# The end of a two-layer transformer kernel: the last head period and the final norm and projection rearranged

## The reference

```python
# 32 heads, causal top-k mask; x is 1024 x 512
attn = jax.nn.softmax(scores, axis=-1)
out = jnp.einsum('bhqk,bhkd->bqhd', attn, v).reshape(b, s, H * VD)
x = x + out @ o_w
# last part: one 512 x 512 matrix, W with its low-rank terms folded in
x = x + (layernorm(x) @ (W + lora).T + bias)
```

## Time and profile before

| what | value |
|---|---|
| median of 3 runs | 1490.97 us (1489.38 to 1497.5) |
| profiled execution: its time | 1491.74 us |
| its span, first to last instruction | 1489.9 us |
| mean granted TensorE clock over the span | 0.946 |

### The profile page before, as it was taken

One profiled execution on the slowest core, in us unless ns is written; L12 is line 12 of the kernel. 1 busy time (PEld: TensorE's weight loads), 2 busy tenths in 40 slices (PEclk: granted clock), 3 DMA queues, 4 the chain that ended last, 5 costly groups with the idle time before them and its releaser, 6 DMA issues.

```text
span 1489.9 us, 21223 instructions
## 1 busy us (share of the span) xinstructions
PE 1329.6 (89%) x7144; PEld 1109.1 (74%) x7144; DVE 1113.9 (75%) x2247; ACT 823.4 (55%) x1799; POOL 629.7 (42%) x620
## 2 busy tenths in 40 slices
PE   2767999999899789997659999999999999999978
PEld 1645788888789677774358788888888888888856
DVE  5637434443657599999948988988989988898864
ACT  4554442233246466763446776666777667667631
POOL 2421110010037445544435555556665555555522
PEclk9978999999999899996579999999999999999988
DMA  6531210000212335645530000000000000000101
GB/s 217 173 99 50 88 61 1 1 19 0 66 39 70 103 88 169 211 140 182 177 113 13 1 28 28 27 28 27 27 2 28 27 28 27 28 27 15 55 25 57
DMA packets 83722, 95.59 MB, mean 64 GB/s; under 512 B 11680, under 2 KB 59296, under 8 KB 83104
## 3 DMA queue, kind: packets, MB, share of 16 engines
q1 hardware_dynamic: 83616, 94.24, 20.1%
HBM read 75.34 MB, written 18.87 MB: 63 GB/s over the span
## 4 chain that ended last, share of the span: by engine, by line
PE 66%; DVE 17%; ACT 4%; DMA 4%; issue 3%; SPq 2%; POOL 2%; DVEq 1%; ACTq 0%; POOLq 0%
PE ps L328 16%; PE ps L330 15%; PE ps L329 15%; PE ps L1691 8%; PE ps L1711 3%; DVE acc L1274 3%; PE ps L1710 3%; DVE top L1285 2%; DVE xn_l L1339 2%; DVE rop L1297 1%; DVE acc L1288 1%; DVE rop L1295 1%; DVE pm L1327 1%; DMA iwq_raw<-in_L_attn_idx_wq_w 1%; DMA wring<-in_L_ffn_w 1%
## 5 line engine op out<-in xcount | busy, mean ns | idle before, releaser
L682 POOL TENSOR_SCALAR pm<-pm,smx 128x128 f32<-128x128 f32 (+7 forms) x256 | 189.7, 750 | 218.6 <-DVE smx L1333 218.6
L1327 DVE CUSTOM_DVE_ANT_0 pm<-ps,mbias 128x128 f32<-128x128 f32 (+7 forms) x256 | 191.5, 753 | 40.8 <-PE ps L330 25.9
L941 ACT ACTIVATE pm<-pm,smx 128x128 f32<-128x128 f32 (+7 forms) x256 | 197.3, 772 | 35.8 <-DVE smx L1327 34.0
L1691 PE MATMUL ps<-ident,pm 128*128 128x128 f32 x1152 | 176.1, 278 | 9.5 <-DVE xn_l L1339 3.5
L947 ACT ACTIVATE xn_h<-ps 128x512 fp32r<-128x512 f32 (+3 forms) x256 | 128.6, 512 | 86.0 <-PE ps L1691 82.9
L1339 DVE TENSOR_TENSOR xn_l<-ps,xn_h 128x512 fp32r<-128x512 f32 (+3 forms) x256 | 144.6, 588 | 27.3 <-ACT xn_h L947 26.4
L328 PE MATMUL ps<-latT_l,qc_h 128*128 128x512 f32 (+3 forms) x384 | 142.8, 372 | 21.1 <-SPq L319 12.1
L1691 PEld LDWEIGHTS ps<-ident,pm 128*128 128x128 f32 x1152 | 133.2, 142 | 35.9 <-issue 12.7
L330 PE MATMUL ps<-latT_h,qc_h 128*128 128x512 f32 (+3 forms) x384 | 134.0, 349 | 0.0
L329 PE MATMUL ps<-latT_h,qc_l 128*128 128x512 f32 (+3 forms) x384 | 133.4, 347 | 0.0
L1274 DVE SCALAR_TENSOR_TENSOR acc<-ps,iw,acc 128x768 f32<-128x768 f32 (+4 forms) x105 | 87.9, 889 | 24.3 <-ACT ps L855 24.0
(11 more groups left out here) (271 smaller groups left out, 3695.6 us busy)
## 6 DMA issues: line engine op xcount, KB each, us to landing
iwq_raw<-in_L_attn_idx_wq_w SPq DMA_DIRECT2D x48, 256.0 KB, 3.2
base<-in_L_ffn_mean_w SPq DMA_DIRECT2D x28, 256.0 KB, 3.0
wring<-in_L_ffn_w SPq DMA_DIRECT2D x24, 256.0 KB, 3.2
ow_raw<-in_L_attn_o_w SPq DMA_DIRECT2D x8, 512.0 KB, 4.0
xn_t<-in_L_attn_o_w SPq DMA_DIRECT2D x8, 512.0 KB, 4.1
wuvo<-wf_h SPq DMA_DIRECT2D x8, 512.0 KB, 4.1
wuvo<-pr_hl SPq DMA_DIRECT2D x8, 512.0 KB, 3.4
wuvo_h<-wuvo SPq DMA_DIRECT2D x16, 256.0 KB, 2.7
```

What stands on the lines that cost most here:

```text
L682: pool.tensor_scalar(pm[:, i % 4, 0:w], pm[:, i % 4, 0:w], smx[:, 32 + i:33 + i], 0.0, ALU.mult, ALU.add).then_inc(hd_p, 1)
L941: act.activation(pm[:, i % 4, 0:w], pm[:, i % 4, 0:w], ACT.Exp, bias=smx[:, i:i + 1], scale=-1.0, accum_out=smx[:, 16 + i:17 + i]).then_in ...
L1327: dve.tensor_tensor_reduce(out=pm[:, i % 4, 0:w], in0=two_banks(2 * (i % 2), w), in1=mbias[:, TRI[t]:TRI[t + 1]], scale=1.0, scalar=3.0 * BIG,
L1691: done = pe.transpose(ps[:, 4 + i % 2, tile(k)], pm[:, tq % 4, tile(4 * c + k)], ident[:])
```

## The change: what it does

1. **The last period has orders of its own** (`LAST_PE` and so on). The output products of tiles 0 to 3 are split: A (pair 14's part) is put between the last transposes, B (pair 15's part) behind them, both ahead of V3, where Y stood behind V3. The split of tokens 0 to 511 (W0) moves forward in ScalarE's and VectorE's order (V2 ahead of T19). Two of the last transpose groups use banks 3 and 7 in place of 4 and 5.
2. **The last tile of probabilities** is scaled on VectorE (step P15) and no longer on GpSimd; the reciprocal of the tile before it no longer waits for the last exponential.
3. **Norm in three groups** of tiles (0 and 1; 2 and 3; 4 to 7), each with its own statistics, square root and Newton step; the square root's table is loaded right behind the last transposes' evictions.
4. **The scaling for the transposes** moves from VectorE to GpSimd (`last_scale`), in front of or between the bias adds.
5. **Six output banks** for the final products, by `OUT_BANKS`, in place of two; tile sums in eight banks.
6. **No barrier** `meet(e, 2)`; the waits are on the tiles' own semaphores.

No arithmetic is left out, and the count of matmuls is the same.

```diff
+LAST_PE = """T9 S11 T10 V0 S12 T11 T12 S13 T13 V1 T14 S14 T15 S15 T16 T17 V2 T18 T19 A0 T20 A1 T21 A3 T22 T23 A2
+    B0 B1 B2 B3 V3"""
+LAST_DVE = """C4 S10 T8 T9 T10 S11 T11 V0 S12 T12 C5 S13 C6 T13 V1 T14 S14 T15 S15 C7 T16 T17 P15 T18 V2 T19 T20 T21
+    T22 T23"""
+LAST_ACT = """T10 T11 V0 T12 S11 S12 S13 T13 V1 T14 T15 S14 T16 T17 S15 T18 V2 T19 T20 W0 T21 T22 T23"""
+LAST_POOL = "S8 S9 S10 S11 S12 S13 S14 W0"
+
...
-LAST_BANKS = (0, 2, 4, 5)
+SUM_BANKS = (0, 1, 7, 2, 3, 4, 5, 6)
+OUT_BANKS = (7, 2, 3, 4, 5, 6, 7, 2)
 DOWN_FIRST = (7, 4, 5, 6, 0, 2, 1, 3)
...
+
+        def t_bank(p, i):
+            return {20: 3, 21: 7}.get(i, 4 + i % 2) if p == PAIRS - 1 else 4 + i % 2
...
+            def last_scale(t):
+                pool.wait_ge(en_rs, 1 if t < 2 else 2 if t < 4 else 3)
+                if t >= 2:
+                    pool.wait_ge(ln_tr, NT * 3 + t - 1)
+                pool.tensor_scalar(norm_buf(3, t), xt(t), mv[:, t, 0:1], rs_out[:, t:t + 1],
+                                   ALU.subtract, ALU.mult).then_inc(ln_xn, 1)
+
...
+            last_scale(0)
+            last_scale(1)
+            sum_lo(PAIRS - 1, 1)
+            pool.wait_ge(ld_e, 48)
+            last_bias(0)
+            last_scale(2)
+            last_scale(3)
+            last_bias(1)
+            last_bias(2)
+            for t in range(4, NT):
+                last_scale(t)
+                last_bias(t - 1)
+            last_bias(NT - 1)
...
+            act.activation(table[:, 3:4], ones[:, 0:1], ACT.Sqrt)
+            sqrt(6, 2)
+            sum_half(PAIRS - 1, 3)
+            norm_hi(3, 0)
+            sum_hi(PAIRS - 1, 1)
+            norm_hi(3, 1)
+            sqrt(7, 2, 2)
+            norm_hi(3, 2)
+            norm_hi(3, 3)
+            sqrt(8, 4, 4)
+            for t in range(4, NT):
                 norm_hi(3, t)
 
...
+                    elif kind == "P":
+                        dve.wait_ge(hd_exp, 16 * p + i + 1)
+                        dve.reciprocal(smx[:, 32 + i:33 + i], smx[:, 16 + i:17 + i])
+                        dve.drain()
+                        dve.tensor_scalar(pm[:, i % 4, :], pm[:, i % 4, :], smx[:, 32 + i:33 + i], None, ALU.mult)\
+                            .then_inc(hd_last, 1)
...
+            def last_norm(k, first, n):
+                half_norm(k, first, n)
+                dve.drain().then_inc(en_rs, 1)
+
+            def last_out(t):
+                dve.wait_ge(en_bias, t + 1)
+                dve.wait_ge(en_y, t + 1)
+                dve.tensor_tensor(xt(t), xt(t), ps[:, OUT_BANKS[t], :], ALU.add).then_inc(en_o, 1)
+
+            last_add(0)
+            last_stats(0)
+            last_add(1)
+            last_stats(1)
+            last_norm(6, 0, 2)
+            sum_add(PAIRS - 1, 3)
+            last_add(2)
+            norm_lo(3, 0)
+            last_stats(2)
+            norm_lo(3, 1)
+            last_add(3)
+            last_stats(3)
+            last_norm(7, 2, 2)
+            last_add(4)
+            last_stats(4)
+            last_add(5)
+            norm_lo(3, 2)
+            last_stats(5)
+            norm_lo(3, 3)
+            last_add(6)
+            last_stats(6)
+            last_add(7)
+            last_stats(7)
+            last_norm(8, 4, 4)
+            for t in range(NT):
+                if t < 4:
+                    norm_lo(3, t + 4)
+                last_out(t)
```

TensorE's part:

```diff
+                        if c == 0 and (p, tq) == (PAIRS - 1, 15):
+                            pe.wait_ge(hd_last, 1)
+                        elif c == 0:
                             pe.wait_ge(hd_p, 16 * p + tq + 1)
-                        reach(pe, hd_lo, NG * p + i - 1)
+                        if p < PAIRS - 1 or i < 20:
+                            reach(pe, hd_lo, NG * p + i - 1)
+                        elif i == 20:
+                            pe.wait_ge(hd_max, 16 * p + 16)
+                        elif i >= 22:
+                            pe.wait_ge(hd_lo, NG * p + i - 3)
...
+                    elif kind == "A":
+                        pe.wait_ge(hd_olo, 2 * (p - 1) + 1)
+                        if i < 2:
+                            pe.wait_ge(hd_max, 16 * p + 15)
+                        elif i == 2:
+                            pe.wait_ge(hd_lo, NG * p + 22)
+                        else:
+                            pe.wait_ge(hd_max, 16 * p + 16)
+                        products(i, p - 1, SUM_BANKS[i], True, False)
+                    elif kind == "B":
+                        pe.wait_ge(hd_olo, 2 * p + 1)
+                        pe.wait_ge(hd_ldu[p % 2], 32 * (p // 2) + 32)
+                        products(i, p, SUM_BANKS[i], False, True).then_inc(hd_y, 1)
...
+            pe.wait_ge(hd_x, 4 * (PAIRS - 1) + 2)
+            norm_tile(3, 0)
+            norm_tile(3, 1)
+            last_product(0)
             pe.wait_ge(hd_olo, 2 * PAIRS)
...
+            for t in range(4, NT):
+                products(t, PAIRS - 1, SUM_BANKS[t], True, True).then_inc(hd_y, 1)
+            norm_tile(3, 2)
+            norm_tile(3, 3)
+            last_product(1)
+            last_product(2)
+            last_product(3)
+            norm_tile(3, 4)
+            norm_tile(3, 5)
+            for t in range(4, NT):
+                last_product(t)
+                if t < 6:
+                    norm_tile(3, t + 2)
```

More of the change, by code:

```diff
@@ L675, in _, with sum_lo @@
             meet(pool, 1)
+            def sum_lo(p, i):
+                c = slice(512 * i, 512 * i + 512)
+                pool.wait_ge(hd_ohi, 2 * p + i + 1)
+                pool.tensor_tensor(ol_l[:, p % 2, c], ol_f[:, i, :], f(ol_h[:, p % 2, c]), ALU.subtract)\
+                    .then_inc(hd_olo, 1)
             def head_period(period):
-                for kind, i, p in steps(POOL_ORDER, period):
+                for kind, i, p in steps(LAST_POOL if period == PAIRS - 1 else POOL_ORDER, period):
                     if kind == "S":
@@ L1312, in _, with output_add, sum_add @@
             meet(dve, 1)
[L1314 to L1318 removed]
+            def output_add(i, bank):
+                return dve.tensor_tensor(xt(i), xt(i), ps[:, bank, :], ALU.add).then_inc(hd_x, 1)
+            def sum_add(p, i):
+                h, b = divmod(i, 2)
+                r = slice(KR * h, KR * h + KR)
+                dve.wait_ge(hd_ocp, 4 * p + i + 1)
+                dve.tensor_tensor(ol_f[r, b, :], ps[r, 6, :], ol_f[r, b, :], ALU.add).then_inc(hd_of, 1)
             def head_period(period):
[L1321 removed]
+                for kind, i, p in steps(LAST_DVE if period == PAIRS - 1 else DVE_ORDER, period):
                     if kind == "S":
@@ L1660, in _, with products, output @@
             meet(pe, 1)
-            def output(i, p, bank, first, last):
-                for q in ((p - 1, p) if not first and not last else (p,)):
-                    one = mm3(pe, ps[:, bank, :], ol_h[:, q % 2, tile(i)], ol_l[:, q % 2, tile(i)],
-                              wuvo_h[:, q % 2, :], wuvo_l[:, q % 2, :], q == p - 1 or first or last, q == p)
-                one.then_inc(hd_y, 1)
+            def products(i, q, bank, start, stop):
+                return mm3(pe, ps[:, bank, :], ol_h[:, q % 2, tile(i)], ol_l[:, q % 2, tile(i)],
+                           wuvo_h[:, q % 2, :], wuvo_l[:, q % 2, :], start, stop)
+            def output(i, p, bank):
+                if p:
+                    products(i, p - 1, bank, True, False)
+                products(i, p, bank, p == 0, True).then_inc(hd_y, 1)
             def head_period(period):
-                for kind, i, p in steps(PE_ORDER, period):
+                for kind, i, p in steps(LAST_PE if period == PAIRS - 1 else PE_ORDER, period):
                     if kind == "S":
```

129 lines of the change are left out of this document (50 added, 79 removed).

## The result

The changed kernel takes 1483.71 us (median of 19 runs, 1479.9 to 1487.6) against 1490.97 before: ratio 0.9947, 95% interval 0.9938 to 0.9957. By the medians it is 7.3 us faster where 15.0 were forecast. One of the 19 executions of the kernel before took 2593.6 us and is left out of the ratio. In the profiled execution it took 1479.9, the lowest of its 19 runs, so its span alone overstates the gain.

What follows compares the result with a forecast made beforehand. TensorE's tail was taken as the bound, with 22.4 us lost to pauses and low clock. Work of 39.6 plus 5.7 of pauses gave 16.8 us less; minus 1.8 for the clock, 15.0 less: 1476.0 us, range 1472 to 1482.5.

Steps and rivals of the forecast that it cites:

- I take 0.70: Final norm on GpSimd: each 128x512 scaling priced at 0.70 us, from the row for scaling probabilities.
- the upper bound of 1.92: Price of GpSimd's norm scaling from above: the 128x512 mask operation's 1.92 us, set aside for its comparison and bf16 output.
- the rival of dear scaling: Final stage: GpSimd's scaling costs 1.92 us, so only 10.7 us less, time 1480.3; chance 0.15.
- the sum: TensorE's end laid out at full clock: 39.6 us of work plus 5.7 of pauses, span 1473.1, 16.8 us less.
- The slope: Final stage: each 1 us more per GpSimd scaling makes the end 5 us later.
- the table load was free: Square root's table load, behind the last transposes: near 1430.5 with nobody waiting for it; 1.28 us of the old pause.
- no product waited for an output add: Final products: six banks let F1 to F5 wait for no output add; already in the layout's total.
- the whole layout without a fall: T18 to the span's end with the clock high throughout: span 1473.1, time 1474.2; as a rival, chance 0.25.
- the cover behind F1 to F3: F1 to F3 (8.4 us) hide VectorE's work for tiles 4 to 7; pause of 0.1, cover exhausted.
- The clock's share: Just ahead of F0: one fall of TensorE's clock, more likely than not, costing 1.8 us, leaving 15.0 us less.

Runs made afterwards that it cites:

- pool_addmul: Changed kernel with GpSimd's scaling adding a column of minus mean and multiplying, instead of subtracting the mean and multiplying: 1477.81 us, ratio 0.9923.
- pool_muladd: Changed kernel with GpSimd's scaling as multiply by the root's column and add of minus mean times root: 1477.89 us, ratio 0.9912.
- again: The changed kernel run once more without an edit: 1484.37 us, ratio 0.9954.
- dve_again: The changed kernel with the scaling back on VectorE, run a second time without further edit: 1475.07 us, ratio 0.9896.
- act_scale: Changed kernel with the scaling on ScalarE (Identity with scale and bias columns), only bias adds on GpSimd: 1480.9 us, ratio 0.9925.
- dve_scale: Changed kernel with the scaling moved back to VectorE, everything else as changed: 1475.74 us, ratio 0.99.
- mix: Changed kernel with VectorE scaling tiles 0 to 4, GpSimd 5 to 7 by multiply and add, tile 0's split ahead of sum 2's add: 1478.92 us.
- pool_prices: Changed kernel plus twenty 128x512 GpSimd scalings behind its last work, run only for their prices: 1514.02 us in one execution.

## Why the prediction was wrong

**The step that failed** is "I take 0.70" for GpSimd's scaling. It measured 2.07, above even the upper bound of 1.92. With the pair changed to add and multiply, and nothing else on TensorE's path, it measured 0.77 and the kernel came to 1477.81, near the forecast. The row that I took was the nearest by types and shape, and I passed over its pair of operations: probabilities are scaled with multiply and add, the norm with subtract and multiply. The price kernel shows that the pair is what counts. The mask row that I set aside for its comparison (greater-than and multiply, 1.92) was the nearer one: subtract and multiply by constants takes 1.93.

**What that did** is the rival of dear scaling, worked out in the prediction for 1.92. It had a pause of 1.9 behind F0 and 2.8 at N5, a tile on GpSimd as long as one on TensorE, and 10.7 less. Measured are 0.9 to 1.4 at N3, 2.63 at N5, no pause at F0, 3.3 us a tile and tails 10.9, 9.0 and 9.1 less than the 64.84 that the sum was made against. With 0.15 the right case had too small a chance.

That rival stood at 1480.3, and 1483.71 is 3.4 more, above the range's end of 1482.5 too. At 2.07 its own slope makes its 10.7 into 9.9 (16.8 - 5 x 1.37), all at full clock. The tails, in which the clock falls once or twice, give 8.9 against the mean of before's three; the 64.84 of the sum was the longest of them. The medians give 7.3, which is taken up below.

**The slope** of 5 us of end for 1 us of price would make 1.30 x 5 = 6.5 from pool_addmul. The medians give 1483.71 - 1477.81 = 5.9 across two chips, and 6.5 for pool_muladd against `again` on one. The tails give 55.2 - 47.2 = 8.0. I read the tails' excess as what the clock gives back, which I had not counted into the slope: it fell in all three tails of 55.2 and not in the one of 47.2.

**Right by their own numbers:** V3 started 8.13 us behind T18 (1432.29 - 1424.16; laid out 8.14) and ran at full clock. GpSimd could begin to scale 11.5 behind T18 (1435.68 - 1424.16; laid out 11.6). P15 took 0.75 and held up nobody; the table load was free; no product waited for an output add. The tail of the whole layout without a fall, 1473.1 - 1425.06 = 48.0, is met, a little undercut, by the kernels with cheap scaling where the clock did not fall (47.17 and 47.56 on GpSimd, 47.31 on VectorE). So the plan was right, and the cover behind F1 to F3 is thin, as it said: in pool_addmul N4 waits for nothing and N5 0.92, laid out 0.1 and 1.6.

**The clock's share** was put at one fall of 1.8 us at F0. In the changed kernel it falls at F0 in each of three profiles (first matmul 0.61, 0.78, 0.78 instead of 0.47) and at N5 in two of them, and the tails differ by 1.9. With cheap scaling it falls at F0 in dve_again and act_scale, and not in dve_scale, pool_muladd, pool_addmul and mix. Between dve_again and dve_scale, one kernel with the same pauses of 0.82 and 1.39, the fall cost 1.4. So 1.8 was somewhat high for one fall, and what decides whether it comes is not shown. The Trainium skill, TensorE: Matmul & The Clock Gate, section "A second HAM failure mode", speaks, for another kernel, of micro-idles between groups of matmuls that make the clock swing; the traces agree in that it fell only behind pauses, with 0.61 to 0.78 for F0's first matmul behind pauses of 2.36 and 1.34, and 0.47 behind 1.02 and 0.78.

**From the tail to the median.** The tails say 8.9, the medians 7.3, the ratio 7.9 (interval 6.4 to 9.2, from its bounds times 1490.97). Three profiles each and this interval don't contradict one another; what the difference of 1.0 to 1.6 is, if it is any, stays open. It may be the head: T18 starts at 1426.2 in the mean of the eleven profiles with a changed last period and at 1424.5 in before's three. As the eleven spread over 8.6 us, a shift of 1.7 is neither shown nor excluded. The same goes for pool_addmul against dve_scale: equal tails, medians 2 us apart. I can say only that the head varies by more than that from one execution to the next.

## What to carry to other kernels

When an operation is moved to another engine, its price there is read from a row with the same pair of operations, not only the same shape and types; where there is none, the dear row is the value to take. On GpSimd, write the scaling with add and multiply. Before that, ask whether it must move at all: the fastest kernel here is the one in which it stays on VectorE (1475.74 and 1475.07), so that this part of the change, as written, cost 8 to 9 us. Compare kernels by the stretch that the change touches as well as by the total: here the stretch ahead of it varied by more than the change was worth.

## What the runs showed of the hardware

- GpSimd, 128x512 fp32, column or constant operands: pairs of add and multiply 0.62 to 0.77 us, pairs with a subtract 1.93 to 2.08, a single operation 1.57. Where one operation is wanted, a pair with + 0.0 is the cheaper form: the kernel's own scaling of probabilities multiplies by a column and adds 0.0, and takes 0.70, against 1.57 for the multiply alone. Add with multiply cost 0.77 with VectorE idle (pool_prices) and with it busy (pool_addmul).
- The Trainium skill, GPSIMD Engine Reference, section Engine selection, calls one-input work roughly line-rate. VectorE does this scaling in 0.50; the rows agree roughly for add with multiply (0.77, 1.5 times as long) and not for subtract with multiply (2.07, four times).
- ScalarE does the same scaling in 0.76 to 0.81. Yet act_scale's tail is 1.5 us longer than pool_muladd's: F0 starts 0.5 later behind T18 (15.2 against 14.7; N0 and N1 pause 1.21 and 0.74), and the clock fell at F0.
- TensorE's clock was lowered behind pauses of 2.4 and 1.3 us in all three profiles of the changed kernel, and behind pauses of 0.8 and 1.4 us in one of two profiles of the same kernel (dve_scale).
